# Full exponential in place over the scores in PSUM, rounded exponential first, in a decoder layer with softmax attention

## The chip, the cores and the metric

One Trainium2 chip, one of its cores. The time is that of the whole program on the device, in microseconds. The engines of the core are TensorE (PE; its weight loads are shown as PEld), VectorE (DVE), ScalarE (ACT), GpSimd (POOL) and SyncE (SP), which here only issues DMAs.

## What is computed

A decoder layer over 16 sequences of 100 rows of width 128: causal self-attention, cross-attention over 1444 context rows of width 96 with 16 heads, and a quantized feed-forward layer, each with a layer norm ahead and a residual. Nearly all of the time goes into the cross-attention:

```python
h, dh = 16, 64
q = (x @ Wq).reshape(B, Nq, h, dh)
k = (context @ Wk).reshape(B, Nk, h, dh)
v = (context @ Wv).reshape(B, Nk, h, dh)
scores = jnp.einsum('bqhd,bkhd->bhqk', q, k) * (1.0 / sqrt(dh))
attn = jax.nn.softmax(scores, axis=-1)
out = jnp.einsum('bhqk,bkhd->bqhd', attn, v).reshape(B, Nq, h * dh)
return out @ Wo + bo
```

## The kernel before

**Tiling.** The key weights are folded into the queries (M) and the value weights into the output weights (G), so that scores are products of 96-wide queries with the raw context. A batch is one sequence: 1600 queries (16 heads x 100) against 1444 keys in 12 chunks of 128 keys, the last one partly filled. The queries go in two pairs of blocks of 2 x 400 columns. A batch so has 24 steps, step s treating pair s // 12 and one key chunk with 128 x 800 scores; 16 batches make 384 steps.

**High and low parts.** Matrix products run in a rounded format (fp32r). To keep fp32 accuracy each operand is split into a rounded part (hi) and the remainder (lo), and a product is three: hi x hi, lo x hi, hi x lo. A step has six score matmuls (L1075, three terms on two blocks of 400 columns) and six value matmuls (L1107; in the partly filled chunk two, L1091), which treat the step two behind.

**One step on the engines.** TensorE writes the scores into one of two slots of two PSUM banks each, by the step's parity (`ST + 2 * (s % 2)`). ScalarE computes the exponential twice out of this slot: into `pr` in fp32 (L610) and into `pr_hi`, rounded (L613). VectorE computes `pr_lo = pr - pr_hi` (L879); in the partly filled chunk it writes 36 rows of `pr_hi` instead. `pr` has two buffers, `pr_hi` and `pr_lo` have three. TensorE then adds up the values in two further banks.

**Other work in the steps.** A table written out by hand (`AT`) gives each of the 24 steps small pieces of work: 39 row maxima of the next batch's approximate scores (L929 on TensorE, L663 on VectorE, one to four a step from step 1 to step 20), the queries of the next batch (L920, then L568 on ScalarE and L658 `q_lo` on VectorE), the self-attention of the batch after it, and the output projection of the one before (L967, at step 12). They share two PSUM banks in turn; a fill waits until the last use but one of these banks has been read (`misc_free`). In a step TensorE's program holds scores, then values, with the small pieces between them. VectorE's program holds most small pieces ahead of the step's subtraction, so that a late subtraction delays the maxima behind it, and the other way round. L700 is a copy out of such a bank at step 5; L960 is a small product of the self-attention at step 12; L775 on VectorE prepares the last key chunk, right behind the subtraction of step 10.

**GpSimd** works at its own pace in each batch: L488 and L492 (cT_lo, 96 x 758), L505 (a broadcast), L506 (normalizing the output, 96 x 1600) and L498 (cN_lo, 128 x 1056), besides tiny ones such as L475 and L476.

**Waits around the change.** The scores of step n wait at their first matmul until the rounded exponential of step n - 2 is done (`hi_done`). The first exponential waits for the scores and for the subtraction two steps back (`lo_done`), the second for the values three steps back (`pv_done`). The subtraction waits for both exponentials. The value matmuls wait for `hi_done`, and their third term for `lo_done`.

## Time and profile before

| | us |
|---|---|
| median of the runs | 1241.41 |
| lowest and highest of three | 1240.72 to 1242.85 |
| span of the profiled execution | 1241.1 |

The busy shares of the profiled execution are TensorE 93%, its weight loads 84%, VectorE 81%, ScalarE 56% and GpSimd 20%. The profile gives for each group of instructions its line, its engine, what it writes and reads, the count, the busy time and the mean of one; and for idle time of an engine what ended it. In a timeline each row has the start and the duration in us, then engine, line and count; in square brackets stands the idle time of the engine before it. Ends of matmuls are modelled.

### The profile page before, as it was taken

The numbers are of one execution on the slowest core, as the hardware profiler recorded it, in microseconds if no ns is written. First come the engines' busy times: TensorE is split into PE (matmuls) and PEld (weight loads), VectorE is DVE, ScalarE is ACT, GpSimd is POOL, SyncE is SP. The second block draws the span as 40 slices with busy tenths as digits, with TensorE's granted clock in tenths as the row PEclk, the third lists the DMA queues.
The fourth block names the chain that finished last, engine by engine and source line by source line (L and its number), as shares of the span: only waits on it lengthen the run. The fifth ranks groups of instructions, "written<-read, shape, count | busy, mean of one in ns | idle before, by whom it ended". The sixth has DMA issues, their size and how long they took to land.

```text
span 1241.1 us, 20286 instructions
## 1 busy us (share of the span) xinstructions
PE 1159.2 (93%) x6561; PEld 1047.9 (84%) x6561; DVE 1005.4 (81%) x1625; ACT 691.1 (56%) x969; POOL 245.7 (20%) x228
## 2 busy tenths in 40 slices
PE   7789999999999999999999999999999999999997
PEld 5568889898898888888898888989889898988996
DVE  2698888988788798887979878898788889888655
ACT  1245656556464665656556554655556466564653
POOL 3120130302213022130302213130221303022010
PEclk9799999999899999999999999999999999999997
DMA  6101010010101001010000101001010100100000
GB/s 143 38 1 39 1 39 3 6 36 2 39 3 39 4 2 38 4 38 5 16 25 1 39 4 38 3 1 41 3 39 3 39 2 2 40 2 1 3 1 4
DMA packets 12727, 24.40 MB, mean 20 GB/s; under 512 B 4934, under 2 KB 8654, under 8 KB 12494
## 3 DMA queue, kind: packets, MB, share of 16 engines
q1 hardware_dynamic: 12622, 23.00, 6.9%
q8 instruction: 65, 1.06, 0.4%
q14 instruction: 40, 0.33, 0.1%
HBM read 21.88 MB, written 0.82 MB: 18 GB/s over the span
## 4 chain that ended last, share of the span: by engine, by line
PE 77%; issue 10%; DVE 10%; ACT 1%; DMA 1%; DVEq 1%; POOL 0%; SPq 0%; POOLq 0%; ACTq 0%
PE banks L1075 27%; PE banks L1107 26%; PE banks L929 9%; PE banks L967 4%; PE banks L920 4%; DVE pr_lo L879 3%; DVE maxes L663 3%; PE banks L949 1%; DVE cN_hi L775 1%; ACT pr_hi L613 1%; DMA q_hi<-negmaxT 1%; PE banks L1091 1%; PE banks L1010 1%; PE banks L960 1%; PE banks L1038 1%
## 5 line engine op out<-in xcount | busy, mean ns | idle before, releaser
L610 ACT ACTIVATE pr<-banks 128x800 f32<-128x800 f32 x384 | 322.4, 840 | 442.4 <-PE banks L1075 438.3
L879 DVE TENSOR_TENSOR pr_lo<-pr,pr_hi 128x800 fp32r<-128x800 f32 x352 | 424.0, 1205 | 61.2 <-ACT pr_hi L613 54.1
L663 DVE TENSOR_REDUCE maxes<-banks 128x1 f32<-128x482 f32 x585 | 372.5, 653 | 51.0 <-PE banks L929 45.9
L613 ACT ACTIVATE pr_hi<-banks 128x800 fp32r<-128x800 f32 x384 | 319.1, 831 | 0.0
L929 PE MATMUL banks<-cT_hi,q_hi 96*128 96x482 f32 x585 | 228.4, 390 | 27.5 <-DVE maxes L663 18.1
L1075 PE MATMUL banks<-q_hi,cT_hi 97*128 97x400 f32 x768 | 215.6, 362 | 9.1 <-DMA q_hi<-negmaxT 6.9
L1075 PE MATMUL banks<-q_hi,cT_lo 96*128 96x400 f32 x768 | 208.5, 352 | 0.0
L1075 PE MATMUL banks<-q_lo,cT_hi 96*128 96x400 f32 x768 | 203.9, 346 | 0.0
L1107 PE MATMUL banks<-pr_hi,cN_hi 128*97 128x400 f32 x704 | 187.7, 348 | 0.0
L1107 PE MATMUL banks<-pr_lo,cN_hi 128*97 128x400 f32 x704 | 186.9, 347 | 0.6 <-DVE pr_lo L879 0.6
L1107 PE MATMUL banks<-pr_hi,cN_lo 128*96 128x400 f32 x704 | 186.3, 346 | 0.0
L1075 PEld LDWEIGHTS banks<-q_hi,cT_hi 97*128 97x128 f32 x768 | 135.2, 191 | 20.6 <-ACT pr_hi L613 6.4
L929 PEld LDWEIGHTS banks<-cT_hi,q_hi 96*128 96x128 f32 x585 | 109.9, 188 | 50.3 <-DVE maxes L663 26.2
L1075 PEld LDWEIGHTS banks<-q_lo,cT_hi 96*128 96x128 f32 x768 | 143.2, 190 | 0.0
L1075 PEld LDWEIGHTS banks<-q_hi,cT_lo 96*128 96x128 f32 x768 | 139.2, 190 | 3.3
L475 POOL TENSOR_TENSOR ve<-mv,eps 100x1 f32<-100x1 f32 x48 | 9.2, 192 | 616.6 <-DVE mv L642 616.6
L1107 PEld LDWEIGHTS banks<-pr_lo,cN_hi 128*97 128x97 f32 x704 | 115.0, 164 | 16.5 <-DVE pr_lo L879 1.1
L1107 PEld LDWEIGHTS banks<-pr_hi,cN_lo 128*96 128x96 f32 x704 | 114.5, 163 | 15.9
L1107 PEld LDWEIGHTS banks<-pr_hi,cN_hi 128*97 128x97 f32 x704 | 114.3, 164 | 12.5
L506 POOL TENSOR_TENSOR o_sb<-o_sb,rball 96x1600 f32<-96x1600 f32 x15 | 55.6, 3706 | 105.8 <-issue 105.8
L920 PEld LDWEIGHTS banks<-x2T,M 128*96 128x96 f32 x512 | 56.8, 175 | 7.6 <-DVE maxes L663 1.4
L920 PE MATMUL banks<-x2T,M 128*96 128x100 f32 x512 | 59.6, 263 | 2.2 <-DVE maxes L663 1.1
(117 smaller groups left out, 888.3 us busy)
## 6 DMA issues: line engine op xcount, KB each, us to landing
cT_raw<-in_ctxT SPq DMA_DIRECT2D x16, 568.5 KB
cN_raw<-in_ctx SPq DMA_DIRECT2D x16, 528.0 KB
out<-result SPq DMA_DIRECT2D x16, 50.0 KB
X<-in_x SPq DMA_DIRECT2D x1, 700.0 KB
cN_raw<-in_ctx_last SPq DMA_DIRECT2D x16, 40.5 KB
wqT<-in_wqT SPq DMA_DIRECT2D x1, 512.0 KB, 5.4
wo<-in_wo SPq DMA_DIRECT2D x1, 512.0 KB, 13.3
wkT<-in_wkT SPq DMA_DIRECT2D x1, 384.0 KB, 7.0
```

The costliest lines, as they stand in the source:

```text
L506: nc.gpsimd.tensor_tensor(out=o_sb[0:DC, :], in0=o_sb[0:DC, :], in1=rball[:, :], op=ALU.mult).then_inc(on_done, 1)
L610: nc.scalar.activation(pr[:, s % 2, :].rearrange("p (a q) -> p a q", a=2), pair, ACT.Exp, scale=float(DH) ** -0.5).then_inc(exp_done, 1)
L613: nc.scalar.activation(pr_hi[:, s % RING, :].rearrange("p (a q) -> p a q", a=2), pair, ACT.Exp, scale=float(DH) ** -0.5).then_inc(hi_done, 1)
L663: nc.vector.tensor_reduce(maxes[:, t, p:p + 1], here[:, 0:PW], AX.X, ALU.max).then_inc(misc_free, 1)
L775: nc.vector.scalar_tensor_tensor(out=cN_hi[par][0:ROWS, FULL, 0:DC], in0=last_hi[:, :].bitcast(F32), scalar=last[0:ROWS, 0:1], in1=cN_raw[ ...
L879: nc.vector.tensor_tensor(low[rows, s % RING, :], pr[rows, s % 2, :], pr_hi[rows, s % RING, :].bitcast(F32), ALU.subtract).then_inc(lo_don ...
L920: mm = nc.tensor.matmul(here[0:DC, i * S:(i + 1) * S], M[:, h, :], x2T[par][:, :], start=True, stop=True)
L929: mm = nc.tensor.matmul(here[:, 0:PW], q_hi[par][0:DC, qtile(t):qtile(t) + P], cT_hi[par][0:DC, PAT[p]:PAT[p] + PW], start=True, stop=True)
L949: mm = nc.tensor.matmul(here[:, m * S:(m + 1) * S], wself[:, m, :], xnT[par][:, :], start=True, stop=True)
L967: mm = nc.tensor.matmul(here[0:S, 0:D], o_sb[0:DC, h * S:(h + 1) * S], G[:, h, :], start=(h == 0), stop=(h == H - 1))
L1075: mm = nc.tensor.matmul(banks[:, ST + 2 * (s % 2) + a, 0:BLK], k, q[:, q0:q0 + BLK], start=(i == 0), stop=(i == 2))
L1107: mm = nc.tensor.matmul(banks[0:m, OUT + a, 0:BLK], k, e[:, r, a * BLK:(a + 1) * BLK], start=False, stop=(s % NCH == NCH - 1 and i == 2))
```

## The change

ScalarE computes the rounded exponential first (into `pr_hi`). Then it computes the full one in place: it reads the slot of scores in PSUM and writes it there. VectorE subtracts `pr_hi` from the slot in PSUM, and the SBUF buffer `pr` is gone, with its wait for `lo_done` on ScalarE. Since the slot now holds data until the subtraction has read it, the scores of step n wait for `lo_done` of step n - 2 and no longer for `hi_done`.

```diff
-        pr = sb("pr", [P, 2, PAIR])
...
                     act.wait_ge(st_ready, n + 1)
-                    at_least(act, lo_done, n - 1)
-                    nc.scalar.activation(pr[:, s % 2, :].rearrange("p (a q) -> p a q", a=2), pair, ACT.Exp,
-                                         scale=float(DH) ** -0.5).then_inc(exp_done, 1)
                     at_least(act, pv_done, n - RING + 1)
                     nc.scalar.activation(pr_hi[:, s % RING, :].rearrange("p (a q) -> p a q", a=2), pair, ACT.Exp,
                                          scale=float(DH) ** -0.5).then_inc(hi_done, 1)
+                    nc.scalar.activation(pair, pair, ACT.Exp, scale=float(DH) ** -0.5).then_inc(exp_done, 1)
...
-                    nc.vector.tensor_tensor(low[rows, s % RING, :], pr[rows, s % 2, :],
-                                            pr_hi[rows, s % RING, :].bitcast(F32), ALU.subtract).then_inc(lo_done, 1)
+                    slot = ST + 2 * (s % 2)
+                    nc.vector.tensor_tensor(low[rows, s % RING, :].rearrange("p (a q) -> p a q", a=2),
+                                            banks[rows, slot:slot + 2, 0:BLK],
+                                            pr_hi[rows, s % RING, :].bitcast(F32).rearrange("p (a q) -> p a q", a=2),
+                                            ALU.subtract).then_inc(lo_done, 1)
...
                 if i == 0:
-                    at_least(pe, hi_done, b * STEPS + s - 1)
+                    at_least(pe, lo_done, b * STEPS + s - 1)
```

On ScalarE, in two steps of the first batch, with the waits in square brackets, before:

```order
L610 ACTIVATE pr<-banks 128x800 [waits lo_done,st_ready]
L613 ACTIVATE pr_hi<-banks 128x800 [waits pv_done]
L568 ACTIVATE q_hi<-banks 96x400 [waits misc_ready]
L562 ACTIVATE cN_hi<-cN_raw 128x4x96
L610 ACTIVATE pr<-banks 128x800 [waits lo_done,st_ready]
L613 ACTIVATE pr_hi<-banks 128x800 [waits pv_done]
```

and with the change:

```order
L609 ACTIVATE pr_hi<-banks 128x800 [waits pv_done,st_ready]
L611 ACTIVATE banks<-banks 128x2x400
L567 ACTIVATE q_hi<-banks 96x400 [waits misc_ready]
L561 ACTIVATE cN_hi<-cN_raw 128x4x96
L609 ACTIVATE pr_hi<-banks 128x800 [waits pv_done,st_ready]
L611 ACTIVATE banks<-banks 128x2x400
```

The rounded exponential has moved ahead of the full one, which now writes the banks that it reads; the other work keeps its place.

On TensorE, around the start of the scores of a step, before:

```order
L929 MATMUL banks<-cT_hi,q_hi 128x482 [waits misc_free]
L1107 MATMUL banks<-pr_hi,cN_hi 97x400 [waits hi_done]
L1107 MATMUL banks<-pr_hi,cN_hi 97x400
L1107 MATMUL banks<-pr_hi,cN_lo 96x400 x2
L1107 MATMUL banks<-pr_lo,cN_hi 97x400 [waits lo_done]
L1107 MATMUL banks<-pr_lo,cN_hi 97x400
L929 MATMUL banks<-cT_hi,q_hi 128x482 [waits misc_free]
L1075 MATMUL banks<-q_hi,cT_hi 128x400 [waits hi_done]
```

and with the change:

```order
L929 MATMUL banks<-cT_hi,q_hi 128x482 [waits misc_free]
L1107 MATMUL banks<-pr_hi,cN_hi 97x400 [waits hi_done]
L1107 MATMUL banks<-pr_hi,cN_hi 97x400
L1107 MATMUL banks<-pr_hi,cN_lo 96x400 x2
L1107 MATMUL banks<-pr_lo,cN_hi 97x400 [waits lo_done]
L1107 MATMUL banks<-pr_lo,cN_hi 97x400
L929 MATMUL banks<-cT_hi,q_hi 128x482 [waits misc_free]
L1075 MATMUL banks<-q_hi,cT_hi 128x400 [waits lo_done]
```

Nothing has moved on TensorE; the last row, the first matmul of the scores, waits for another semaphore.

## Rows read from the trace of the kernel before

**Rows 1.** The page's first part: busy us, share of the span, instructions.

```profile
PE 1159.2 (93%) x6561; PEld 1047.9 (84%) x6561; DVE 1005.4 (81%) x1625; ACT 691.1 (56%) x969; POOL 245.7 (20%) x228
```

**Rows 2.** Groups (busy us, mean ns | idle before) and two lines (ns min/median/max).

```profile
L879 DVE TENSOR_TENSOR pr_lo<-pr,pr_hi 128x800 fp32r<-128x800 f32 x352 | 424.0, 1205 | 61.2 <-ACT pr_hi L613 54.1 <-issue 3.9 <-ACT pr L610 1.8
L663 DVE TENSOR_REDUCE maxes<-banks 128x1 f32<-128x482 f32 x585 | 372.5, 653 | 51.0 <-PE banks L929 45.9
...
L658 DVE TENSOR_TENSOR q_lo<-banks,q_hi x64: 498/570/573, 27.7 to 1117.8; 96x400 fp32r<-96x400 f32 x64
...
L613 ACT ACTIVATE pr_hi<-banks x384: 824/831/837, 60.5 to 1223.4; 128x800 fp32r<-128x800 f32 x192
```

**Rows 3.** Waits of TensorE's matmuls: waited for, total us, times, longest us.

```profile
PE banks L929 <- DVE maxes L663: 18.1, 21, 3.1
PE banks L960 <- DVE maxes L663: 15.2, 13, 2.8
PE banks L946 <- DVE xn L647: 7.8, 5, 5.1
PE banks L929 <- DVE V L700: 7.5, 14, 0.6
```

**Rows 4.** Timeline (start us, duration us), steps 10 to 12 of the seventh batch.

```profile
535.82 4.14 POOL L506 TENSOR_TENSOR o_sb<-o_sb,rball 96x1600 f32<-96x1600 f32 x1 [6.82 <-issue]
...
538.11 2.70 DVE L879 TENSOR_TENSOR pr_lo<-pr,pr_hi 128x800 fp32r<-128x800 f32 x1
...
539.91 3.01 POOL L498 TENSOR_TENSOR cN_lo<-cN_raw,cN_hi 128x1056 fp32r<-128x1056 f32 x1
...
540.73 2.30 DVE L775 SCALAR_TENSOR_TENSOR cN_hi<-last_hi,last,cN_raw 108x96 fp32r<-108x96 f32 x1
...
543.66 0.46 PE L960 MATMUL banks<-V,prT 100*100 100x128 f32 x2 [2.80 <-DVE maxes L663]
```

**Rows 5.** Timeline, steps 4 and 5 of the same batch.

```profile
518.35 1.82 POOL L492 TENSOR_TENSOR cT_lo<-cT_raw,cT_hi 96x758 fp32r<-96x758 f32 x1 [7.05 <-DMA rrow<-rsums]
...
519.08 1.94 DVE L879 TENSOR_TENSOR pr_lo<-pr,pr_hi 128x800 fp32r<-128x800 f32 x1
...
521.28 0.48 PE L929 MATMUL banks<-cT_hi,q_hi 96*128 96x482 f32 x1 [0.55 <-DVE V L700]
```

**Rows 6.** Timeline: VectorE instructions that read PSUM beside a GpSimd instruction.

```profile
536.36 0.65 DVE L663 TENSOR_REDUCE maxes<-banks 128x1 f32<-128x482 f32 x1
...
877.68 0.55 POOL L476 TENSOR_TENSOR rs<-ve,minus_half 100x1 f32<-100x1 f32 x1
...
877.74 0.57 DVE L658 TENSOR_TENSOR q_lo<-banks,q_hi 96x400 fp32r<-96x400 f32 x1 [0.41 <-ACT q_hi L568]
```

**Rows 7.** Timeline: a subtraction and the weight load that starts behind it, four places.

```profile
510.56 1.60 DVE L879 TENSOR_TENSOR pr_lo<-pr,pr_hi 128x800 fp32r<-128x800 f32 x1
...
511.25 0.41 PEld L1075 LDWEIGHTS banks<-q_hi,cT_hi 97*128 97x128 f32 x2
...
552.98 0.98 DVE L879 TENSOR_TENSOR pr_lo<-pr,pr_hi 128x800 fp32r<-128x800 f32 x1
...
553.90 0.42 PEld L1075 LDWEIGHTS banks<-q_hi,cT_hi 97*128 97x128 f32 x2
...
1172.79 0.99 DVE L879 TENSOR_TENSOR pr_lo<-pr,pr_hi 128x800 fp32r<-128x800 f32 x1 [0.93 <-ACT pr_hi L613]
...
1174.02 0.37 PEld L1075 LDWEIGHTS banks<-q_hi,cT_hi 97*128 97x128 f32 x2
...
1174.20 0.53 PE L1075 MATMUL banks<-q_hi,cT_hi 97*128 97x400 f32 x2
...
1224.34 0.99 DVE L879 TENSOR_TENSOR pr_lo<-pr,pr_hi 128x800 fp32r<-128x800 f32 x1 [1.20 <-ACT pr_hi L613]
...
1225.39 0.25 PEld L1107 LDWEIGHTS banks<-pr_lo,cN_hi 128*97 128x97 f32 x2 [0.18 <-DVE pr_lo L879]
```

**Rows 8.** A window: us, then busy us by engine, granted clock (PEclk), DMA share, GB/s.

```profile
318.00:328.00 10.00, 7.18 (x32) 6.39 (x31) 7.35 (x10) 1.63 (x3) 4.04 (x4) 0.66 0.39 116
```

More of the change, by code:

```diff
@@ L184, in decoder_layer @@
         m_done, g_done = sem("m_done"), sem("g_done")
-        exp_done, hi_done = sem("exp_done"), sem("hi_done")
+        hi_done, exp_done = sem("hi_done"), sem("exp_done")
         o_evac = sem("o_evac")
```

## The prediction

> **What bounds the kernel now.** I read the busy shares first, then the matmul engine's waits, and then the timeline of one batch. TensorE is busy 93% of the span, VectorE 81%, ScalarE only 56% [rows 1]. So a gain must come out of the TensorE idle time, and freeing VectorE counts only where TensorE waits for it. The waits say that it does: four releasers, all on VectorE, hold up matmuls for 18.1, 15.2, 7.8 and 7.5 us [rows 3]. Of the 7.8 one wait of 5.1 us is longer than the other four can be together, and I leave it out (it is no wait for a subtraction; the remaining 2.7 us are four waits). That leaves 43.5 us in 21 + 13 + 4 + 14 = 52 waits. Two weight loads take 0.37 us and two matmuls 0.53 us from end to end [rows 7], so matmuls follow each other every 0.18 us while one is drawn 0.34 us long; an idle stretch between drawn rows really cost 0.16 us more: 52 x 0.16 = 8.3 us. **Together 51.8 us.**
>
> Why VectorE is late can be read from one instruction. The subtraction pr_lo takes 0.98 to 0.99 us where it is undisturbed [rows 7], but 1.205 in the mean [rows 2]: 352 x (1.205 - 0.985) = 77 us of stretching. The stretched ones meet a GpSimd instruction. In [rows 4] GpSimd's product runs from 535.82 to 539.96; the subtraction starts at 538.11 and ends at 540.81, 0.85 us after it. In [rows 5] GpSimd ends at 520.17, the subtraction at 521.02: again 0.85 us later. So it stands still until GpSimd is through. The next VectorE instruction, L775, meets the next GpSimd instruction and takes 2.30 us, and the matmul L960 has by then waited 2.80 us. In [rows 5] the stretched subtraction holds the copy that frees the bank of L929, and TensorE waits 0.55 us.
>
> **The subtraction's operand in PSUM.** Both inputs of pr_lo lie in SBUF. VectorE instructions that read PSUM do not stand still: a maximum (L663) at 536.36 lies whole under the GpSimd product and takes 0.65 us, its mean over 585 [rows 2, 6]. The closest relative of the new form is q_lo, which subtracts an SBUF operand from a PSUM one: its longest of 64 is 0.573 us [rows 2], also at 877.74, where GpSimd's L476 runs from 877.68 to 878.23 [rows 6]; blocked as above, it would have ended some 0.44 us after that, at 878.67, and it ended at 878.31. That is thin evidence (L476 is a tiny instruction), hence a rival below. The Trainium skill, page "SBUF — State Buffer", section "Who interferes with whom", says that a VectorE instruction with two SBUF inputs is fully blocked by a GpSimd one that reads SBUF, and that one with at most one SBUF input is not. By it the stretching would vanish altogether; the rows on two SBUF inputs agree, and no row here shows an 800-element subtraction from PSUM.
>
> Its unblocked duration: q_lo needs 0.498 to 0.573 us for 400 elements, 0.65 for a maximum over 482 [rows 2]. Two points give (0.653 - 0.570) / 82 = 1.01 ns an element, so 800 elements come to 0.90 to 0.98 us. The SBUF form takes 0.98 to 0.99 [rows 7]. I take 0.98, the nearest row: no change unblocked. Against the change speaks the Trainium skill, page "Perfetto Trace Analysis", section "Optimizing Scalar/DVE Operations": about 60 ns of overhead on SBUF and 125 on PSUM for VectorE. By it each of 384 subtractions would be 0.065 us longer and the sum below some 2 us worse (28 waits at steps 3 and 15).
>
> What the unblocked subtraction returns, by place:
> - Steps 5 (14 waits on L700), 7 and 11 (most of the 21 on L663), 12 (13 on L960) and 3 (xn). At each the delay of the subtraction ahead of it (1.94 - 0.98 = 0.96 us in rows 5, 2.70 - 0.98 = 1.72 us in rows 4) is larger than TensorE's wait, or, in rows 4, together with L775's 2.0 us. So the whole wait goes: 51.8 us.
> - Not reached: waits of the first batch that have nothing to do with pr_lo (about 4 us), and L775, which keeps both inputs in SBUF. It now starts near 539.1 while GpSimd's product still runs, and waits up to 0.9 us; I put 3 us on that. **Gain: 51.8 - 7 = 45 us.**
> - Behind one of the other 2.8 us waits the granted clock fell: it is 0.66 over the ten us around it [rows 8], so part of them ran at the lower level (1.2 GHz), worth 10 x (1 - 0.66) = 3.4 us. Before it fell TensorE had been waiting, and in [rows 4] the same wait had no such sequel. **Gain: 3 us.**
>
> **The slot is held longer.** This is the price. Scores of step n + 2 overwrite the two banks of step n. They waited for the high exponential, and now wait for the subtraction (lo_done). A released weight load starts 0.06 us after the subtraction's end: 1224.34 + 0.99 = 1225.33, load at 1225.39 [rows 7]. Then:
> - Step 3: the subtraction at 510.56 would end at 511.54 unblocked, the weight load could start at 511.60 and stood at 511.25: 0.35 us lost. In 14 batches: 4.9 us.
> - Step 15: the subtraction ends at 552.98 + 0.98 = 553.96, load possible at 554.02, was at 553.90: 0.12 us, 15 times: 1.8 us.
> - A step with twelve matmuls and nothing else, as in the last batch, is the tightest regular case: subtraction end 1172.79 + 0.99 = 1173.78, load possible at 1173.84, was at 1174.02: 0.18 us to spare, no cost. A handful of last-batch steps with other VectorE work ahead: 1.3 us.
> **Cost: 8 us.** Behind the waiting weight load everything of TensorE is queued; ScalarE then starts its exponentials later, which has 44% idle time as cover.
>
> **The two exponentials.** 384 pairs, order swapped. The subtraction needs both, so it starts as before. The high one comes 0.84 us earlier, for which nobody waits (a value matmul runs two steps behind). The old waits for lo_done and pv_done on ScalarE are met anyway. The new one reads and writes PSUM in place; no row has a ScalarE write to PSUM. Bounds: 0.83 us, the same instruction into SBUF (L613) [rows 2], and twice that, if reading and writing one bank took turns. Below 0.83 is possible and would only add to the 0.18 us to spare. I take 0.83, because rate is set by elements in every other row; the other end is a rival.
>
> **Sum** against the profiled execution: 1241.1 - 45 - 3 + 8 = 1201.1 us of span; the median of the runs is 0.3 us above that span, so 1201.4 us.
>
> **Rivals.**
> - *Gain falls short* (same mechanism). With the big waits gone the next thing is late: two banks pass maxima from TensorE to VectorE, and VectorE keeps about 930 us of work (1005 - 77) in a shorter span. If half of the 45 us come back as shorter waits, 45 / 2 - 8 + 3 = 17 us are left: 1224. For it: steps with three or four maxima need 4 x 0.65 + 0.98 = 3.6 us of VectorE. Against: in each place VectorE gains more than TensorE does. 20%.
> - *The subtraction is still blocked*, because its other input and its output stay in SBUF. Then nothing is returned, and the new gate puts every stretch in front of the scores: step 3 loses 510.56 + 1.60 + 0.06 - 511.25 = 0.97 us x 14 = 13.6 us, steps 11 and 12 some 0.7 us a batch that their later wait doesn't absorb, 10 us: 1241.4 + 24 = 1265. It decides when the stretched ones stay above about 1.3 us. 6%.
> - *The in-place exponential is slow.* Everything above 0.18 us extra goes into the slot's cycle, half of it per step. At 0.83 us extra: 0.33 us in about 12 light steps of 15 batches, 59 us: 1201 + 59 = 1260. It outweighs the gain from some 0.6 us extra on. 7%.
> - *No change that can be measured*: both effects cancel, 1239 to 1244. 3%.
>
> **How the numbers follow.** Forecast 64% (1188 to 1212; below: all 51.8 + 3 us returned and costs near zero), short gain 20% (1212 to 1238), nothing 3%, slower 13%. A measurement of this kernel can tell 0.2% (2.5 us) from no change. Faster: 0.64 + 0.20 = 0.84; same 0.03; slower 0.13. The range 1188 to 1232 leaves out the 13% and 3%, a few per cent of the short gains and few below: some 2 in 10.
>
> **What would show it.** Right: the subtraction's maximum near 1.0 us; no wait of TensorE for L700's successor, and those for maxima down to a few us; a new wait of the scores' weight load for the subtraction, some 30 times, 0.1 to 0.4 us; granted clock without the dips at step 12. Wrong: subtractions that end 0.85 us after a GpSimd instruction (blocked); the second exponential over 1.0 us; waits for maxima that stay above 20 us (short gain).

## The result and the profile after

The changed kernel takes 1184.15 us in the median of four runs (1180.66 to 1188.88), the one before 1241.58 in the same round of runs (1240.72 to 1242.85). The ratio is 0.9533, with a 95% interval of 0.9503 to 0.9564: 57.4 us, or 4.7%, less. The forecast was 1201.4 with a range from 1188. The direction and the cause came true; the time lies 4 us below the range, and the gain was 57 us where 40 had been forecast.

The page of the changed kernel: busy time, share of the span and instructions of each engine, then further down the shares of the chain of work that ended last.

```profile
PE 1141.1 (96%) x6561; PEld 1043.3 (88%) x6561; DVE 931.6 (79%) x1625; ACT 692.8 (59%) x969; POOL 231.7 (20%) x228
...
PE 90%; DVE 5%; issue 3%; ACT 1%; DMA 1%; POOL 0%; DVEq 0%; SPq 0%; POOLq 0%; ACTq 0%
```

Against [rows 1] VectorE lost 73.8 us of busy time and GpSimd 14.0, though both execute as many instructions as before. Both had been standing still inside instructions (the last section has GpSimd's). ScalarE is the same to 2 us: the swap of the exponentials costs it nothing. TensorE's own busy time is 18 us less, because rows drawn across a wait, or at the lower clock, are longer, and both have become rare. Of the chain that ended last TensorE now holds 90%; in the page of before it held 77%, with 10% for VectorE and 10% for issue.

```profile
PE 77%; issue 10%; DVE 10%; ACT 1%; DMA 1%; DVEq 1%; POOL 0%; SPq 0%; POOLq 0%; ACTq 0%
```

(That line is of the kernel before.) The three instructions that were changed, after, by line: shortest, median and longest in ns, first and last start in us.

```profile
L877 DVE TENSOR_TENSOR pr_lo<-banks,pr_hi x352: 968/982/993, 65.2 to 1167.0; 128x800 fp32r<-128x800 f32 x176
...
L609 ACT ACTIVATE pr_hi<-banks x384: 834/840/845, 59.3 to 1165.4; 128x800 fp32r<-128x800 f32 x192
...
L611 ACT ACTIVATE banks<-banks x384: 828/833/848, 60.0 to 1166.1; 128x800 f32<-128x800 f32 x192
```

These rows decide three of the prediction's questions. The longest of 352 subtractions takes 993 ns, where the mean of before was 1205 [rows 2]: none is stretched any more. That is not because they now miss GpSimd: 84 of them overlap one of its large instructions and 37 lie wholly inside one, where before 71 overlapped and none lay inside. Undisturbed it is as long as from SBUF. And the in-place exponential, of which no row of before told, takes 833 ns, as L613 did [rows 2].

The places of [rows 4] after the change (L505 is the old L506, L877 the old L879, L497 the old L498, L772 the old L775), seventh batch, start and duration in us:

```profile
513.42 3.63 POOL L505 TENSOR_TENSOR o_sb<-o_sb,rball 96x1600 f32<-96x1600 f32 x1 [7.04 <-issue]
...
515.52 0.98 DVE L877 TENSOR_TENSOR pr_lo<-banks,pr_hi 128x800 fp32r<-128x800 f32 x1
...
516.42 0.76 DVE L772 SCALAR_TENSOR_TENSOR cN_hi<-last_hi,last,cN_raw 108x96 fp32r<-108x96 f32 x1
...
517.03 2.28 POOL L497 TENSOR_TENSOR cN_lo<-cN_raw,cN_hi 128x1056 fp32r<-128x1056 f32 x1
...
518.11 0.38 PE L960 MATMUL banks<-V,prT 100*100 100x128 f32 x2
```

The subtraction runs from 515.52 to 516.50 wholly inside the GpSimd product, and neither waits for the other: the product takes 3.63 us where it took 4.14 in this batch, cN_lo 2.28 where it took 3.01. L960 no longer waits; before, it did for 2.80 us. L772, which kept both inputs in SBUF, still stands still until shortly after the product's end (517.05), but for 0.45 us and not 2.0, because it here meets one GpSimd instruction and not two in a row. Over all batches it is no better off: before, 4 of its 16 were stretched (8.0 us in all), now 13 are (10.8 us), because the subtraction ahead of it no longer ends after GpSimd. The median went from 308 to 754 ns.

The place of [rows 5]:

```profile
496.54 1.82 POOL L491 TENSOR_TENSOR cT_lo<-cT_raw,cT_hi 96x758 fp32r<-96x758 f32 x1 [6.95 <-DMA rrow<-rsums]
...
497.32 0.98 DVE L877 TENSOR_TENSOR pr_lo<-banks,pr_hi 128x800 fp32r<-128x800 f32 x1
498.22 0.28 DVE L697 COPY V<-banks 100x128 f32<-100x128 f32 x1
...
498.82 0.38 PE L929 MATMUL banks<-cT_hi,q_hi 96*128 96x482 f32 x1
```

The copy follows the subtraction at once, and L929 starts without a wait.

TensorE's waits, matmuls and then weight loads, after: waited for, total us, times, longest us.

```profile
PE banks L1075 <- DMA q_hi<-negmaxT: 6.8, 5, 2.5
PE banks L946 <- DVE xn L644: 6.3, 2, 4.9
...
PE banks L960 <- DVE maxes L660: 3.5, 3, 1.2
PE banks L929 <- DVE maxes L660: 2.4, 3, 1.8
```

```profile
PEld banks L1075 <- DVE pr_lo L877: 6.9, 17, 1.9
...
PEld banks L960 <- DVE maxes L660: 4.5, 3, 1.5
PEld banks L929 <- DVE maxes L660: 3.5, 3, 2.2
PEld banks L946 <- DVE xn L644: 1.7, 1, 1.7
```

And the weight loads' waits in the kernel before, a view that the prediction did not use:

```profile
PEld banks L929 <- DVE maxes L663: 26.2, 23, 3.4
PEld banks L960 <- DVE maxes L663: 19.5, 13, 3.2
PEld banks L929 <- DVE V L700: 12.4, 14, 0.9
PEld banks L946 <- DVE xn L647: 7.1, 11, 1.7
```

The four releasers of [rows 3] hold up weight loads for 26.2 + 19.5 + 12.4 + 7.1 = 65.2 us before, and for 3.5 + 4.5 + 0.6 + 1.7 = 10.3 us after (the 0.6 is one wait for the copy L697 in the first batch): **54.9 us** returned, close to the whole gain. What the change adds are waits for the subtraction at L1075, 17 in all: fourteen of 0.23 to 0.34 us at step 3, one in each middle batch, two in the last batch, and one of 1.9 us at the start of a batch, where the kernel before waited as long under another name.

To see where the time went step by step, I took from both traces the start of each step's scores and summed the interval from one step to the next over the 14 middle batches. The steps that moved by more than 0.5 us, in us:

| scores of step, to the next | before | after | difference |
|---|---|---|---|
| 0 | 42.5 | 40.0 | -2.5 |
| 2 | 23.6 | 25.4 | +1.8 |
| 3 | 48.7 | 45.4 | -3.3 |
| 5 | 59.2 | 48.5 | -10.7 |
| 7 | 51.4 | 39.9 | -11.5 |
| 8 | 48.5 | 47.1 | -1.4 |
| 11 | 42.6 | 36.9 | -5.7 |
| 12 | 110.6 | 89.2 | -21.4 |
| 23 | 38.1 | 37.4 | -0.7 |
| all of the 14 batches | 1028.3 | 973.2 | -55.1 |

The first batch gave 2.1 us and the last lost 0.2. The gain is where the prediction had put it, in steps 3, 5, 7, 11 and 12; one step became longer. The 2.5 us at step 0 are no wait: two stretches of lower clock in the trace of before, at 726.8 and 873.6 us, lie there.

### The profile page after: what moved, and what is told of

Same layout as the page of the kernel before. It is cut to its first block, busy times and chain, and to the rows that moved or that the text cites. A ratio compares the mean times of both kernels' runs of the same rounds, so it can differ in the third digit from the quotient of the medians.

```text
span 1183.6 us, 20273 instructions
## 1 busy us (share of the span) xinstructions
PE 1141.1 (96%) x6561; PEld 1043.3 (88%) x6561; DVE 931.6 (79%) x1625; ACT 692.8 (59%) x969; POOL 231.7 (20%) x228
## 4 chain that ended last, share of the span: by engine, by line
PE 90%; DVE 5%; issue 3%; ACT 1%; DMA 1%; POOL 0%; DVEq 0%; SPq 0%; POOLq 0%; ACTq 0%
PE banks L1075 34%; PE banks L1107 30%; PE banks L929 11%; PE banks L967 4%; PE banks L920 4%; PE banks L949 1%; PE banks L1091 1%; DVE pr_lo L877 1%; DVE maxes L660 1%; PE banks L1010 1%; PE banks L1000 0%; DMA q_hi<-negmaxT 0%; PE banks L1038 0%; PE banks L979 0%; DVE cN_hi L772 0%
## 5 line engine op out<-in xcount | busy, mean ns | idle before, releaser
L609 ACT ACTIVATE pr_hi<-banks 128x800 fp32r<-128x800 f32 x384 | 322.4, 840 | 398.7 <-PE banks L1075 398.7
L877 DVE TENSOR_TENSOR pr_lo<-banks,pr_hi 128x800 fp32r<-128x800 f32 x352 | 346.8, 985 | 67.3 <-ACT banks L611 66.6
L611 ACT ACTIVATE banks<-banks 128x800 f32<-128x800 f32 x384 | 319.9, 833 | 0.0
L929 PE MATMUL banks<-cT_hi,q_hi 96*128 96x482 f32 x585 | 224.2, 383 | 4.8 <-DVE maxes L660 2.4
L1075 PE MATMUL banks<-q_hi,cT_hi 97*128 97x400 f32 x768 | 217.0, 364 | 8.9 <-DMA q_hi<-negmaxT 6.8
L1075 PE MATMUL banks<-q_hi,cT_lo 96*128 96x400 f32 x768 | 208.0, 352 | 0.0
L1075 PE MATMUL banks<-q_lo,cT_hi 96*128 96x400 f32 x768 | 204.2, 347 | 0.0
L1075 PEld LDWEIGHTS banks<-q_hi,cT_hi 97*128 97x128 f32 x768 | 132.4, 191 | 25.7 <-issue 8.5
L1075 PEld LDWEIGHTS banks<-q_lo,cT_hi 96*128 96x128 f32 x768 | 143.2, 190 | 0.0
L1075 PEld LDWEIGHTS banks<-q_hi,cT_lo 96*128 96x128 f32 x768 | 138.4, 189 | 3.8
L1107 PEld LDWEIGHTS banks<-pr_lo,cN_hi 128*97 128x97 f32 x704 | 114.2, 162 | 15.4
L1107 PEld LDWEIGHTS banks<-pr_hi,cN_hi 128*97 128x97 f32 x704 | 113.7, 163 | 12.4
L929 PEld LDWEIGHTS banks<-cT_hi,q_hi 96*128 96x128 f32 x585 | 109.9, 188 | 16.4 <-DVE q_lo L655 4.6
L505 POOL TENSOR_TENSOR o_sb<-o_sb,rball 96x1600 f32<-96x1600 f32 x15 | 54.6, 3641 | 106.3 <-issue 72.0
```

The costliest lines, as they stand in the source:

```text
L505: nc.gpsimd.tensor_tensor(out=o_sb[0:DC, :], in0=o_sb[0:DC, :], in1=rball[:, :], op=ALU.mult).then_inc(on_done, 1)
L609: nc.scalar.activation(pr_hi[:, s % RING, :].rearrange("p (a q) -> p a q", a=2), pair, ACT.Exp, scale=float(DH) ** -0.5).then_inc(hi_done, 1)
L611: nc.scalar.activation(pair, pair, ACT.Exp, scale=float(DH) ** -0.5).then_inc(exp_done, 1)
L877: nc.vector.tensor_tensor(low[rows, s % RING, :].rearrange("p (a q) -> p a q", a=2), banks[rows, slot:slot + 2, 0:BLK], pr_hi[rows, s % RI ...
L929: mm = nc.tensor.matmul(here[:, 0:PW], q_hi[par][0:DC, qtile(t):qtile(t) + P], cT_hi[par][0:DC, PAT[p]:PAT[p] + PW], start=True, stop=True)
L1075: mm = nc.tensor.matmul(banks[:, ST + 2 * (s % 2) + a, 0:BLK], k, q[:, q0:q0 + BLK], start=(i == 0), stop=(i == 2))
```

## The experiments

The theory: VectorE's subtraction stood still behind GpSimd because both of its inputs lay in SBUF; an input in PSUM frees it; the price is that the slot of scores stays taken until the subtraction has read it. The rivals: the gain came from the order of the exponentials, or from the room in the slot, or it would be reached in another way altogether.

All results, in us, each with the kernel before on the same chip:

| kernel | median | before | ratio and 95% interval |
|---|---|---|---|
| b_gate: before, scores wait for the subtraction | 1255.03 | 1244.2 | 1.0098 (1.0056 to 1.0139) |
| b_swap: before, rounded exponential first | 1238.16 | 1244.2 | 0.9965 (0.9933 to 0.9998) |
| b_cut: before, GpSimd's large work cut | 1177.71 | 1244.2 | 0.9456 (0.9437 to 0.9476) |
| a_cut: changed, the same cut | 1182.07 | 1244.2 | 0.9494 (0.9471 to 0.9517) |
| b_cut_gate: b_cut and b_gate together | 1183.59 | 1240.81 | 0.9536 (0.9511 to 0.9561) |
| a_l775_8: changed, last_chunk two steps earlier | 1181.62 | 1240.81 | 0.9517 (0.9492 to 0.9542) |
| a_idle8: changed, 0.2 us more ScalarE a step | 1184.45 | 1240.81 | 0.9541 (0.9509 to 0.9573) |
| a_idle384: changed, 0.52 us more ScalarE a step | 1197.42 | 1240.81 | 0.9647 (0.9615 to 0.968) |
| after2: the changed kernel again | 1183.69 | 1242.69 | 0.9535 (0.9499 to 0.957) |
| b_cut2: b_cut again | 1178.05 | 1242.69 | 0.9489 (0.9458 to 0.952) |
| b_cut_gate2: b_cut_gate again | 1182.61 | 1242.69 | 0.9524 (0.9493 to 0.9555) |
| a_max20: a_l775_8, maxima spread otherwise | 1188.09 | 1242.69 | 0.9565 (0.9534 to 0.9596) |

### The price alone: b_gate

The kernel before, with nothing of the change but its wait.

```diff
                 if i == 0:
-                    at_least(pe, hi_done, b * STEPS + s - 1)
+                    at_least(pe, lo_done, b * STEPS + s - 1)
```

> The kernel before with one edit: the scores of step n wait for the subtraction of step n - 2 instead of its rounded exponential. Nothing else of the change. Theory (the change gains because subtractions no longer stand behind GpSimd; the longer-held slot costs little only because of that): here they still stand behind it, so the slot is dear. Step 3 loses up to 512.16 + 0.05 - 511.25 = 0.96 us in 14 batches, steps 11 and 12 some more that their later wait for maxima partly absorbs: 1250 to 1265 us. Rival (the slot costs next to nothing in any case, since TensorE waits for the same subtraction a little later anyway): 1241 to 1245 us.

1255.03 us, 10.8 slower than before and inside what was expected. The wait is there: the two rows are of its matmuls and its weight loads, the third of the subtraction.

```profile
PE banks L1075 <- DVE pr_lo L879: 26.1, 31, 1.7
...
PEld banks L1075 <- DVE pr_lo L879: 43.7, 46, 2.0
```

```profile
L879 DVE TENSOR_TENSOR pr_lo<-pr,pr_hi x352: 971/991/3357, 65.3 to 1237.4; 128x800 fp32r<-128x800 f32 x176
```

The new wait takes 43.7 us, but the kernel loses only 10.8. At step 2 the interval grows from 23.6 to 34.0 us, at step 10 from 36.8 to 47.3 and at step 11 from 42.6 to 44.7, together 23 us; step 12 shrinks from 110.6 to 101.7 and step 3 from 48.7 to 45.5, together 12 us, which are waits that came a little later anyway. What is left of the 43.7 was delay of weight loads that did not delay the matmuls as much: their own rows have 26.1. So the later holding of the slot is a cost, and the gain of the change comes from something else. It also gives the size of the rival "still blocked": 11 us, where the prediction had 24.

### The order alone: b_swap

The kernel before with the rounded exponential first, both still into SBUF. The scores wait for whichever is second, as before.

```diff
                     act.wait_ge(st_ready, n + 1)
-                    at_least(act, lo_done, n - 1)
-                    nc.scalar.activation(pr[:, s % 2, :].rearrange("p (a q) -> p a q", a=2), pair, ACT.Exp,
-                                         scale=float(DH) ** -0.5).then_inc(exp_done, 1)
                     at_least(act, pv_done, n - RING + 1)
                     nc.scalar.activation(pr_hi[:, s % RING, :].rearrange("p (a q) -> p a q", a=2), pair, ACT.Exp,
                                          scale=float(DH) ** -0.5).then_inc(hi_done, 1)
+                    at_least(act, lo_done, n - 1)
+                    nc.scalar.activation(pr[:, s % 2, :].rearrange("p (a q) -> p a q", a=2), pair, ACT.Exp,
+                                         scale=float(DH) ** -0.5).then_inc(exp_done, 1)
...
                 if i == 0:
-                    at_least(pe, hi_done, b * STEPS + s - 1)
+                    at_least(pe, exp_done, b * STEPS + s - 1)
```

> The kernel before with the two exponentials in the other order, both still written to SBUF; the scores wait for the second of them, as they did. Theory: nobody waits for the rounded exponential, 1241 us within 2. Rival (a part of the gain is due to the rounded exponential coming 0.84 us earlier): 1235 us or less.

1238.16 us: the ratio is 0.35% below 1 (the medians lie 6.0 us apart), with an interval that ends just under 1. That is less than the theory's 1241 within 2 and more than the rival's 1235: neither was met. The order brings a few of the 57 us, some 6 at most by the medians, and half of the 6 is the granted clock (0.983 in the mean against 0.981 on that chip). The waits for maxima are still there, and the subtraction is stretched up to 3442 ns. The weight loads' waits:

```profile
PEld banks L929 <- DVE maxes L663: 31.2, 29, 3.3
PEld banks L960 <- DVE maxes L663: 13.2, 13, 1.0
```

Why the waits at L960 became shorter (19.5 to 13.2 us) and those at L929 longer (26.2 to 31.2) I did not follow up.

### The cause taken away: b_cut, a_cut

GpSimd's five large instructions of a batch (two halves of cT_lo, cN_lo, the broadcast and the product) are cut to 8 columns, in the kernel before and in the changed one. The low parts are set to zero once at the start and the outputs are not normalized, so both kernels leave that work out. The same edit in both:

```diff
-                nc.gpsimd.tensor_tensor(out=cT_lo[par][:, 0:half], in0=cT_raw[:, 0:half],
-                                        in1=cT_hi[par][0:DC, 0:half].bitcast(F32), op=ALU.subtract)
+                nc.gpsimd.tensor_tensor(out=cT_lo[par][:, 0:8], in0=cT_raw[:, 0:8],
+                                        in1=cT_hi[par][0:DC, 0:8].bitcast(F32), op=ALU.subtract)
...
-                nc.gpsimd.tensor_tensor(out=cN_lo[par][:, :, :], in0=cN_raw[:, 0:FULL, :],
-                                        in1=cN_hi[par][:, 0:FULL, 0:DC].bitcast(F32), op=ALU.subtract).then_inc(cNlo_done, 1)
+                nc.gpsimd.tensor_tensor(out=cN_lo[par][:, 0, 0:8], in0=cN_raw[:, 0, 0:8],
+                                        in1=cN_hi[par][:, 0, 0:8].bitcast(F32), op=ALU.subtract).then_inc(cNlo_done, 1)
...
-                order.link(nc.gpsimd.partition_broadcast(rball[:, :], rrow[:, :]))
-                nc.gpsimd.tensor_tensor(out=o_sb[0:DC, :], in0=o_sb[0:DC, :], in1=rball[:, :],
+                order.link(nc.gpsimd.partition_broadcast(rball[:, 0:8], rrow[:, 0:8]))
+                nc.gpsimd.tensor_tensor(out=o_sb[0:DC, 0:8], in0=o_sb[0:DC, 0:8], in1=rball[:, 0:8],
                                         op=ALU.mult).then_inc(on_done, 1)
```

> The kernel before with GpSimd's five large instructions of a batch cut to 8 columns (the low parts of the context are then zero and the outputs are not normalized: this work is left out). VectorE's subtraction still reads two SBUF operands. Theory (the whole gain is the standing still behind GpSimd): 1183 to 1192 us, and the subtraction's longest under 1.1 us. Rival (reading PSUM or writing it by ScalarE brings a good part by itself): over 1200 us.

> The changed kernel with the same cut of GpSimd's work (left out as there). Theory: only L772, which still has two SBUF inputs, can gain, and the waits at step 12 behind it are 3.5 us in three batches, so 1176 to 1183 us, a gain of 2 to 8 us where the same cut gives the kernel before over 50. Rival: the cut gains here what it gains in the kernel before, some 1130 us.

b_cut takes 1177.71 us, 66.5 less than before on that chip and 5 below what was expected, with the subtraction still reading two buffers in SBUF. a_cut takes 1182.07, 4.4 us above b_cut. The changed kernel (1184.15, on another chip) lies only 2 us above a_cut; by the intervals of the 14 middle batches it is 5.3 (973.2 and 967.9 us), 4.7 of it at step 12. So GpSimd's large instructions cost the kernel before 65 us and the changed one 2 to 5: the change takes away nearly all of what they cost, and the 4.4 between a_cut and b_cut are the change's own price. In b_cut2, the same kernel again, two SBUF inputs are harmless once GpSimd has little to do:

```profile
L880 DVE TENSOR_TENSOR pr_lo<-pr,pr_hi x352: 971/983/1231, 66.0 to 1158.0; 128x800 fp32r<-128x800 f32 x176
```

### The price without the blocking: b_cut_gate, b_cut2, b_cut_gate2

b_cut with the one line of b_gate; the last two repeat both on one chip, because the difference is a few us.

```diff
                 if i == 0:
-                    at_least(pe, hi_done, b * STEPS + s - 1)
+                    at_least(pe, lo_done, b * STEPS + s - 1)
```

> The kernel before with GpSimd's large instructions cut as in b_cut (that work is left out), and in addition the scores wait for the subtraction. Against b_cut this is the price of the longer-held slot alone, where no subtraction stands still. The prediction's term: 8 us more than b_cut, 1186. The trace of the changed kernel says less: only step 3 waits in every batch, some 0.13 us of the step's period, 2 to 3 us in all: 1179 to 1181. If a_cut's distance from b_cut (4 us) is this price, it lies at 1181 to 1183.

> The kernel of b_cut once more (GpSimd's large instructions cut, that work left out), as the base for the next one on the same chip: 1176 to 1180 us, so some 5 us under the changed kernel, although its subtraction reads only SBUF.

> The kernel of b_cut_gate once more (the same work left out). Against b_cut2 it is the price of the longer-held slot. The prediction had 8 us; a_cut lay 4.4 us over b_cut on one chip, and the trace of the changed kernel says 2 to 3. I expect 4 to 6: 1181 to 1184. Were it 8 or more, the prediction's term would be right and the missing 17 us would all have to lie in the waits that were returned.

b_cut_gate took 1183.59 us, just above what was expected, on another chip than b_cut. On one chip it is 1182.61 - 1178.05 = **4.6 us**, where the prediction had 8. The step intervals put it at the same places as in the changed kernel: step 2, 23.6 to 25.4 us; step 3, 44.5 to 45.4; the last batch 57.0 to 58.4. Step 15, to which the prediction gave 1.8 us, is 34.1 in both. Step 0 too reads 3.1 us more in both traces with the longer-held slot (43.1 against 40.0 in b_cut2). That is not its price: each of the two traces caught two stretches of lower clock there, b_cut has one (41.1), and a_cut, which holds the slot as long, has none (40.0). Over the six runs of each, b_cut2 and b_cut_gate2 were granted the same clock, 0.987. But the 4.6 us, small as they are, are best read within a us or two. With b_gate there are now all four corners:

| | scores wait for the exponential | scores wait for the subtraction |
|---|---|---|
| GpSimd blocks VectorE | 1244.2 (before) | 1255.0 (+10.8) |
| GpSimd's work cut | 1178.1 | 1182.6 (+4.6) |

(The upper row is of one chip, the lower of another, where before took 1242.7.) The changed kernel, at 1183.7 on the second chip, lies 1.1 us from the lower right corner.

Why the price is small is in one place of the changed kernel, step 3 of the seventh batch:

```profile
488.89 0.98 DVE L877 TENSOR_TENSOR pr_lo<-banks,pr_hi 128x800 fp32r<-128x800 f32 x1
...
489.69 0.38 PE L929 MATMUL banks<-cT_hi,q_hi 96*128 96x482 f32 x1
...
489.93 0.30 PEld L1075 LDWEIGHTS banks<-q_hi,cT_hi 97*128 97x128 f32 x2 [0.23 <-DVE pr_lo L877]
489.93 0.64 PE L1075 MATMUL banks<-q_hi,cT_hi 97*128 97x400 f32 x2
```

The subtraction ends at 489.87, the weight load starts 0.06 us later, as predicted. But the first matmul is drawn to start with it, at 489.93, while in [rows 7] it stands 0.18 us behind its load (1174.02 and 1174.20). Part of the load's lead was spare. The place loses only the 0.03 us by which the matmul is late after L929 (one is due about 0.21 us after the start of the other) and the 0.11 by which its pair is longer (0.64 for 0.53): 0.14, not 0.35. In the 14 batches steps 2 and 3 lose 1.8 + 0.9 = 2.7 us, or 0.19 a batch.

### What was left of the old wait: a_l775_8

L772 still has two SBUF inputs. It is moved from behind step 10 to behind step 8, where no large GpSimd instruction runs.

```diff
-                    if s == 10 and present(b, 1):
+                    if s == 8 and present(b, 1):
                         last_chunk(b + 1, 1 - par)
```

> The changed kernel with last_chunk (L772, the one large VectorE instruction that still has two SBUF inputs) behind the subtraction of step 8 instead of step 10, where GpSimd is between its broadcast and its product. Theory: L772 no longer stands still (about 0.31 us each, 0.75 in the median and 2.4 at most before), and the waits at step 12 behind it (L960, 3.5 us in three batches, some 4 us with the 0.16 each) go: 2 to 5 us less than the changed kernel. Rival: GpSimd's instructions come at another time and it stands still there too, no change.

1181.62 us, within what was expected. All 16 are now undisturbed:

```profile
L772 DVE SCALAR_TENSOR_TENSOR cN_hi<-last_hi,last,cN_raw x16: 307/310/311, 48.8 to 1061.8; 108x96 fp32r<-108x96 f32 x16
```

In the changed kernel the longest was 2414 ns. The interval of step 12 falls from 89.2 to 84.5 us over 14 batches, what b_cut2 has without GpSimd's work, and the wait at L960 is gone; all other steps stay within 0.4 us. So what was left at L775, which the prediction had put at 3 us, is 4.7. By the runs alone, 1181.62 against 1184.15 and 1183.69 on other chips, this version is not told apart from the changed kernel; the trace tells it. It is the best complete version that I have.

### How much room the slot has: a_idle8, a_idle384

What would a slow in-place exponential have cost? Nothing slow can be made of it, but an instruction between the two exponentials delays the second and the subtraction in the same way. First 8 columns:

```diff
                     nc.scalar.activation(pr_hi[:, s % RING, :].rearrange("p (a q) -> p a q", a=2), pair, ACT.Exp,
                                          scale=float(DH) ** -0.5).then_inc(hi_done, 1)
+                    nc.scalar.activation(idle[:, 128 * (s % 4):128 * (s % 4) + 8], ident[:, 0:8], ACT.Copy)
                     nc.scalar.activation(pair, pair, ACT.Exp, scale=float(DH) ** -0.5).then_inc(exp_done, 1)
```

then 384:

```diff
-                    nc.scalar.activation(idle[:, 128 * (s % 4):128 * (s % 4) + 8], ident[:, 0:8], ACT.Copy)
+                    nc.scalar.activation(idle[:, s % 4, :, :],
+                                         ident[:, :].unsqueeze(1).to_broadcast([P, 3, P]), ACT.Copy)
```

> The changed kernel with a ScalarE instruction of 8 columns, used by nobody, between the two exponentials of each step. It delays the full exponential, so the subtraction and the release of the slot, by some 0.2 us, and measures the room in the slot's cycle. The prediction put the room of the lightest regular step at 0.18 us, and each microsecond above it at half a microsecond a step. By that this costs steps 3 and 15 0.2 us each, 28 times, and nearly nothing elsewhere: 5 to 8 us over the changed kernel. If the room is larger, as matmuls that follow the subtraction's end by 0.15 us without loss suggest, 3 to 5 us.

> The same with 384 columns, some 0.5 us. The prediction's rule: (0.5 - 0.18) / 2 = 0.16 us in 12 light steps of 15 batches, 29 us, and 0.3 us more at step 3: 1184 + 29 + 4 = 1217. With a room of 0.3 us instead: 0.1 x 180 = 18 us and 7 at steps 3 and 15: 1209. Rival (steps wait so seldom for the slot that ScalarE's idle time hides it): under 1190.

The instruction takes 0.20 us in a_idle8, and in a_idle384:

```profile
L612 ACT ACTIVATE idle<-ident x384: 511/515/532, 60.4 to 1179.6; 128x384 f32<-128x384 f32 x192
```

0.20 us at each of 384 steps costs nothing that can be told (1184.45), where 3 to 8 us had been expected. The further 0.32 us cost 13.0: 0.034 us a step, a tenth of what was added. The result lies between the two that were expected, 1209 or more and under 1190. The prediction's rule failed in both. By it, half of every excess over 0.18 us in 12 steps of each batch, a_idle384 should have lost 0.32 / 2 x 12 x 15 = 29 us more than a_idle8. It did not lose them there: in the 14 middle batches steps 13 to 19, 21 and 22 moved by 0.3 us or less each. What moved is step 2 (25.9 to 28.4 us), step 20 (43.0 to 46.3), step 23 (38.4 to 39.7), the last batch (58.3 to 60.0) and step 0 (40.0 to 43.6, of which some 3 are two stretches of lower clock); steps 1 and 12 moved by 1.1 and -1.3. So in most steps the slot has more room than 0.52 us. That other work between the matmuls makes it is the likely reason; that the last batch, whose steps hold little else, lost some fits it.

### Where TensorE still waits: after2, a_max20

after2 is the changed kernel once more, as the base on this chip. a_max20 is a_l775_8 with the 39 maxima of a batch spread over steps 1 to 19, so that they, and the transfer that needs them, end before the last step.

```diff
-        MAXES = [0, 2, 1, 1, 1, 2, 2, 3, 2, 3, 2, 2, 1, 4, 2, 1, 2, 1, 2, 2, 3]
+        MAXES = [0, 2, 1, 1, 1, 2, 2, 3, 2, 3, 2, 2, 2, 4, 2, 2, 2, 2, 2, 2]
```

> The changed kernel once more, beside the others on one chip. 1180 to 1187 us.

> The changed kernel with last_chunk behind step 8, and the 39 maxima of a batch spread over steps 1 to 19 instead of 1 to 20, so that the row maxima reach the queries one step earlier. VectorE has room for it now. The waits of the scores for the DMA q_hi<-negmaxT (8.0 us in six, 1.1 to 1.7 us each plus one at the start) should go but for the one at the start: 5 to 7 us under a_l775_8, 1175 us. Rival: steps 14 to 19 have two maxima each and their subtraction comes later, so the scores wait for the slot instead: 1181 us or more.

after2: 1183.69 us, as the changed kernel had taken before. a_max20: 1188.09, where 1175 was expected: 4.4 us slower than after2 on its chip, and 6.5 slower than a_l775_8 on another. The rival had the direction, but not the reason. Against a_l775_8, step 20 gives 7.8 us back (42.9 to 35.1) and step 1 2.3, but step 15 takes 6.8 more (34.2 to 41.0), step 12 5.4 (84.5 to 89.9), step 17 3.0 and step 23 1.9. The maxima that were moved there hold the two banks that the transpose of xn (L963) and the product with G (L967) also need. Waits of the weight loads:

```profile
PEld banks L963 <- DVE maxes L660: 5.3, 13, 0.4
...
PEld banks L967 <- DVE maxes L660: 3.8, 13, 0.3
```

And what the moved maxima were to remove, the waits that the view puts down to the transfer of the maxima (8.0 us in a_l775_8), stayed, under other names (waits of matmuls in a_max20):

```profile
PE banks L1075 <- DVE pr_lo L877: 5.2, 4, 1.6
PE banks L1075 <- issue: 2.6, 2, 1.5
PE banks L1075 <- DMA q_hi<-negmaxT: 2.5, 1, 2.5
```

Beside one at the start of the program (2.5 us) and one of 0.4 in the last batch, these are five waits at the start of every second batch, 1.1 to 1.6 us each; in a_l775_8 the same five have 0.9 to 1.3. The transfer is not their cause: around 550 us it is issued 7 us before the wait ends, in a_l775_8 5 us, and the wait is no shorter. Nor is the subtraction that is named for three of them: the kernel before has the same five waits (1.0 to 1.5 us), and its scores do not wait for the subtraction. The loop turns there, which makes it the likely cause; I did not test that.

## Why the prediction fell short

Step by step, in its own order:

- **What bounds the kernel**: right. TensorE idle time that VectorE's late work had caused is what came back, at steps 3, 5, 7, 11 and 12.
- **The cause**: right. Cutting GpSimd's work in the kernel before (b_cut) returns what the change does and 6 to 9 us more (its price and what L775 still loses), and swapping the exponentials alone (b_swap) about a tenth of it at most.
- **The PSUM operand is not blocked, and no slower**: right. 968 to 993 ns in 352 instructions, 84 of them beside a large GpSimd one. The Trainium skill, page "SBUF — State Buffer", section "Who interferes with whom", had said the first; the trace agrees, now for the 800-element subtraction too. The page "Perfetto Trace Analysis" of the Trainium skill, section "Optimizing Scalar/DVE Operations", has VectorE's overhead at 60 ns on SBUF and 125 on PSUM; the medians here are 983 ns (both inputs in SBUF, b_cut2) and 982 ns (one in PSUM), so for this instruction the row decides against the page.
- **The returned waits: a term mis-sized, and the main failure.** The prediction had 51.8 us, less 7 for what is "not reached", so 45. It sized them from the idle time between matmul rows with 0.16 us added for each. The weight loads' rows give 65.2 before and 10.3 after: 54.9 us. The deduction was about right (10.3 us remain, of which 4.5 at L960 are L772's; a_l775_8 measured 4.7), but it was taken from a total that was too low. Step 5 shows by how much each way of counting errs. In a typical batch its interval shrank by 0.82 us (4.30 to 3.48). The matmuls' idle time there is 0.55, with the correction 0.71; the weight load's wait is 0.90. So the prediction's way counts a seventh too little and the weight loads' a tenth too much.
- **The clock: a term mis-sized.** The prediction counted one dip of the granted clock, [rows 8], for 3 us (3.4 worked out). The trace of before has three more, of 1.7 us each by the same rule, 10 x (1 - 0.83):

```profile
724.00:734.00 10.00, 8.96 (x44) 8.40 (x45) 6.04 (x11) 4.80 (x7) 2.53 (x3) 0.83 0.01 3
870.00:880.00 10.00, 8.51 (x42) 7.55 (x41) 5.08 (x10) 5.19 (x8) 2.51 (x3) 0.83 0.02 3
1125.00:1135.00 10.00, 6.92 (x38) 6.11 (x37) 7.49 (x7) 1.96 (x3) 3.77 (x2) 0.83 0.00 0
```

  Together 8.5 us, and the profiled execution of the changed kernel has none in the middle: over its 60th to 1160th us the granted clock is 1.00.

```profile
60.00:1160.00 1100.00, 1083.72 (x6318) 996.24 (x6318) 893.04 (x1544) 676.78 (x941) 215.76 (x190) 1.00 0.06 17
```

  But one execution is not enough to size this term. Two of the four dips of before (320.7 and 1129.6 us) stand at step 12, behind the long waits; the other two stand at the turn of the loop, where traces with GpSimd's large work cut have such dips too (b_cut one, b_cut_gate two), and after2, the changed kernel again, has one of 6.8 us in its first batch. Every run has its mean granted clock on record: 0.982 over 32 runs of the kernel before, 0.987 over 10 of the changed one, and 0.987 over 10 of b_cut and b_cut2. Since the lower level is half the higher, 1 minus this share, times the span, is the time lost: 22.7 us before, 15.4 after. **7.3 us**, where the prediction had 3.

- **The slot held longer: a term mis-sized.** 8 us against 4.6 (b_cut_gate2 against b_cut2). By place: steps 2 and 3 lose 2.7 us where 4.9 were forecast, step 15 nothing where 1.8 were, the last batch 1.4 where 1.3 were. The release of the weight load 0.06 us behind the subtraction was right. The step that failed was to take each delay of a weight load as a delay of its matmul.
- **The sum** with the measured terms: 54.9 + 7.3 - 4.6 = 57.6 us; the medians differ by 57.4. A check that does not use the waits: with the time lost to the lower clock taken off each run, the means are 1219.6 us before and 1169.3 after, 50.3 apart, and 54.9 - 4.6 is 50.3. That both agree this well is partly luck, for the weight loads' waits count a little too much and the price is good to a us or two. All three errors had the same sign (10, 4 and 3 us), which is why the time fell out of a range that allowed for each of them alone.
- **Rivals.** *Still blocked*: ruled out by the subtraction's 993 ns. *Slow in-place exponential*: ruled out by 833 ns, and its price of 59 us was several times too high, as a_idle384 shows. *Gain falls short*: the waits for maxima did not come back; 10.3 us remain of 65.2. *No change*: ruled out.
- **What would show it.** The forecast of some 30 waits of the scores for the subtraction of 0.1 to 0.4 us each came out as 17, of 0.23 to 0.34 us but for two: one of 0.7 in the last batch and the one of 1.9 at the turn of the loop.

## What to carry to other kernels

Where VectorE and GpSimd work at the same time, look at the longest against the median of each VectorE instruction with two SBUF inputs; if it is several times the median, put one input into PSUM, even at the price of holding the bank longer, and price it by cutting GpSimd's work in a trial. What TensorE won lay between the idle time of its matmul rows and the waits of its weight loads, nearer the latter: take both as bounds, and not the matmul rows alone. Take the granted clock from several executions over the whole span, not from one place of one trace. A delay of a weight load costs only what is left after its lead over the matmul.

## What the runs showed of the hardware

- The blocking holds in both directions: a GpSimd instruction that starts while a subtraction with two SBUF inputs runs is longer too. In the kernel before this holds for all 21 large GpSimd instructions that were lengthened, and for none that was not; a maximum (L663, which reads PSUM) that runs at the start lengthens none. It is cN_lo (L498, now L497) above all. Its median is 3010 ns before and 2288 after; 14 of 16 took about 3.0 us, of which none is left, and that returns 10.2 of the 14.0 us that GpSimd's busy time lost. The product was hardly touched: three of its 15 were longer, the one of [rows 4] (4.14 us) most, and its median is 3643 ns in both kernels. The broadcast was longer in three of 15 (2.5 to 2.7 us for 1.87). The line of cN_lo before, then after:

```profile
L498 POOL TENSOR_TENSOR cN_lo<-cN_raw,cN_hi x16: 2254/3010/3037, 43.7 to 1125.8; 128x1056 fp32r<-128x1056 f32 x16
...
L497 POOL TENSOR_TENSOR cN_lo<-cN_raw,cN_hi x16: 2249/2288/2331, 43.2 to 1072.8; 128x1056 fp32r<-128x1056 f32 x16
```

- An exponential over 128 x 800 takes as long into PSUM, in place, as into SBUF (833 and 831 ns), but the subtraction behind it starts sooner. In the changed kernel:

```profile
490.14 0.83 ACT L611 ACTIVATE banks<-banks 128x800 f32<-128x800 f32 x1
...
491.01 0.99 DVE L877 TENSOR_TENSOR pr_lo<-banks,pr_hi 128x800 fp32r<-128x800 f32 x1 [0.24 <-ACT banks L611]
```

  490.97 to 491.01 is 0.04 us. In the kernel before, where the exponential wrote SBUF:

```profile
1171.87 0.83 ACT L613 ACTIVATE pr_hi<-banks 128x800 fp32r<-128x800 f32 x1
...
1172.79 0.99 DVE L879 TENSOR_TENSOR pr_lo<-pr,pr_hi 128x800 fp32r<-128x800 f32 x1 [0.93 <-ACT pr_hi L613]
```

  1172.70 to 1172.79 is 0.09 us. Over the steps of both traces in which VectorE stood idle before it, the medians are 33 and 89 ns. The 56 ns work for the slot, but they brought the kernel next to nothing: a_cut has them and b_cut_gate has not, and steps 2 and 3 take 25.4 and 45.4 us in both, the last batch 58.1 and 58.4. They are not why the price was below the forecast, for it was measured without them.
- A wait that a view puts down to a transfer kept its length when the transfer was made to end earlier (a_max20). Such a name is a guess until the transfer has been moved.
